# Softmax edge loops of a graph network: two-operand VectorE passes with one operand in PSUM, and two score banks instead of three

## The chip, the core and the metric

The kernel runs on one core of a Trainium2 chip. The core's engines are TensorE (PE, with its weight loads shown as PEld), VectorE (DVE), ScalarE (ACT), GpSimd (POOL) and SyncE (SP); SBUF is the working memory and PSUM the small memory that TensorE writes to. The metric is the device time of one execution in microseconds (us), lower is better.

## The reference

Four graph layers run one after the other on N = 12500 nodes with 64 features and E = 212500 edges sorted by destination. Each layer normalizes the nodes, gathers the source rows along the edges, reduces them per destination, and adds the result to x.

```python
# layer 0: softmax per destination and feature, over the incoming edges
m = relu(feats[src] + edge_h) + EPS
ex = exp(m - segment_max(m, dst)[dst])
a = ex / segment_sum(ex, dst)[dst]
h = segment_sum(m * a, dst)             # then a norm, two linear layers and a batch norm
# layer 1: mean of x[src] per destination, then a linear layer
# layer 2: attention in hyperbolic space (no part of the change)
# layer 3: relational attention, 8 relations x 4 heads
s = leaky_relu(el_all[edge_rel, src] + er_all[edge_rel, dst])
e = exp(s - segment_max(s, dst)[dst])
w = e / segment_sum(e, dst)[dst]
h = segment_sum(feat_all[edge_rel, src] * w, dst)
```

## The kernel before

The edges are padded and cut into two halves, which lie side by side on the partitions (64 features of each half make 128 partitions). A step takes W = 512 edges of each half. There are STEPS = 208 steps in each edge loop. The loops run in series: `softmax_edges(0)`, `mean_edges`, `hyperbolic_edges`, `softmax_edges(3)`, each followed by a stage that works on the nodes. The change touches `softmax_edges` alone, which is built twice: for layer 0 and, with `rel` true, for layer 3.

In every step POOL issues eight indirect DMAs (line 649; four tiles of 128 edges times two halves), each of which gathers 128 rows of a node table by the indices in `idx_all` into one of four slots of `rows`. That makes 1664 gathers in a loop. POOL waits only for the slot: `rows_read` (the same semaphore as `turned`) of four steps before.

The other engines follow, each with its own written-out order of stages with lags in steps:

- PE in layer 0: `to_columns` (lines 764, 766: transposes the rows and the edge features into a bank of `ps_score`), `count` (line 752, counts destinations per bin from `hot`), `to_rows` (line 796, transposes the sums back). In layer 3: `v_columns` (line 775, into `ps_v`), `score_columns` (lines 781 to 788, into `ps_score` and `ps_mult`), `to_rows`.
- DVE in layer 0: `put_in_bins` (line 667), then `segment_sums` of the step two before (lines 713 to 719), then `maxima` of the step before (lines 695 to 707). In layer 3: `own_values` (lines 676, 681), `segment_sums` (lag 3), `maxima` (lag 2).
- ACT: relu or copy of the scores (lines 824, 822), in layer 3 also `widen` (line 813), which waits for the gathered rows; then the exponentials (lines 828, 829), copies out (line 836) and the issue of the stores.
- SP: issues the loads of `attr`, `part_b`, and in layer 3 `v_e` and `marks`.

`maxima` is a running maximum along the edges that starts over at a new destination: `part_b` is 0 inside a segment and very negative where one begins, the scan of line 699 adds it to the running value and takes the maximum with the score, so that `top[:, q, 1:W+1]` holds the maxima after, and `top[:, q, 0:W]` those before, each edge. Lines 704 to 707 then prepare two exponents:

```python
v.tensor_tensor(ps_ex, top[:, q, 0:W], part_b[:, b, :], ALU.add)          # 704
v.tensor_tensor(ex, ps_score[:, c % SCORES, :], top[:, q, 1:W + 1], ALU.subtract)   # 705
v.tensor_tensor(ps_ex, ps_ex, top[:, q, 1:W + 1], ALU.subtract)           # 707
```

`ps_ex` becomes the factor by which the running sums shrink at this edge (zero where a segment begins), `ex` the edge's own weight. `segment_sums` is two scans (716, 719) with `ps_ex` as factor and `ex`, and `ex` times the row, as addends; line 713 makes that product.

Tiles whose names begin with `ps_` lie in PSUM, all others of these loops in SBUF. `slot_free(engine, semaphore, c, ago=n)` makes the engine wait until the step n before has raised the semaphore.

Of the kernel before, what the change touches and what calls it, by code (L numbers as in the profile page):

```python
# [21 lines left out]
ALU = mybir.AluOpType  # L22
ACT = mybir.ActivationFunctionType
# [4 lines left out]
P = 128  # L28
# [48 lines left out]
def build(nc, x, src, dst, edge_attr, edge_type, w0a, b0a, gamma, beta, w0b, b0b, scale0,  # L77
          w1, b1, w2, c2, w3, al3, ar3, b3, out):
    with ExitStack() as whole:
# [455 lines left out]
        def softmax_edges(layer):  # L535
# [3 lines left out]
            rel = layer == 3  # L539
            GW = D + HEADS if rel else D  # L540
            LATER = 1 if rel else 0
            SCORES = 2 if rel else 3
            with nc.cleanup_on_exit(), ExitStack() as ctx:
                def psum(name, shape):
                    return ctx.enter_context(nc.psum_tensor(f"{name}_{layer}", shape, F32))
# [9 lines left out]
                if rel:  # L555
                    v_e = buf("v_e", [P, SLOTS, TILES, HALVES * REL_HEADS])
                    wide = buf("wide", [P, 2, TILES, HALVES * D])
                    marks = buf("marks", [HALVES * REL_HEADS, SLOTS, W, 2], BF16)
                    spread_v = buf("spread_v", [HALVES * REL_HEADS, 2, W])
                    own_v = buf("own_v", [HALVES * REL_HEADS, 2, W])  # L560
                else:
                    attr = buf("attr", [P, SLOTS, HALVES, TILES, D])
# [10 lines left out]
                if not rel:  # L573
                    hot = buf("hot", [P, 2, 2, STREAMS, BLOCKS], BF16)
                    ps_count = psum("ps_count", [P, 2, W])
                    binned, counted, noted = (sem(n) for n in "binned counted noted".split())
                ps_score = psum("ps_score", [P, SCORES, W])
                ps_ex = psum("ps_ex", [P, W])
                ps_out = psum("ps_out", [P, 2, W])
                if rel:  # L580
# [1 line left out]
                    ps_v = psum("ps_v", [HALVES * REL_HEADS, W])  # L582
                got_mask, got_edge, got_rows, put, put_top = ([sem(f"{n}{b}") for b in range(SLOTS)] for n in (
                    "got_mask", "got_edge", "got_rows", "put", "put_top"))
                seeded, v_turned, v_spread, v_own, widened, turned, masked, moved, bent, carried, topped, lowered, diffed, exped, \
                    weighed, summed, back, copied, issue, pe_turn, got_b, parted, powered, merged, m_step, put_cross = (
                        sem(n) for n in (
                            "seeded v_turned v_spread v_own widened turned masked moved bent carried topped lowered diffed exped "
                            "weighed summed back copied issue pe_turn got_b parted powered merged m_step put_cross").split())
                scan_out = scan3 if rel else scan0  # L590
                ROWS = 16 * HALVES * TILES
# [3 lines left out]
                with nc.Block() as block:  # L595
                    @block.sync
                    def _(sp):
                        if rel:
                            first = sp.value_load(cross_i[0:1, 1:2], min_val=0, max_val=HALF - 1)
                            sp.dma_start(spread_v[REL_HEADS:2 * REL_HEADS, 1, W - 1:W],  # L600
                                         at_first[bass.ds(first * HALVES, 1), :].rearrange("a f -> f a"),
                                         allow_slow_non_contiguous=True).then_inc(seeded, 16)

                        def load(c, b, r):
                            if rel:
                                slot_free(sp, v_own, c, ago=SLOTS)
                                sp.dma_start(v_e[:, b, :, :], at_first[bass.ds(c * (W * HALVES), W * HALVES), :].rearrange(
                                    "(p k h) f -> p k (h f)", p=P, k=TILES)).then_inc(got_edge[b], 16)
                                for h in range(HALVES):
                                    sp.dma_start(marks[h * REL_HEADS:(h + 1) * REL_HEADS, b, :, :],  # L610
                                                 mark_row(c + h * STEPS)).then_inc(got_edge[b], 16)
                            else:
                                slot_free(sp, rows_read, c, ago=SLOTS)
                                last = isinstance(c, int) and c == STEPS - 1
                                sp.dma_start(attr[:, b, 0, :, :], edge_rows(edge_attr, c)).then_inc(got_edge[b], 16)
                                sp.dma_start(attr[:, b, 1, :, :], edge_rows(tail, 0) if last else
                                             edge_rows(edge_attr, c + STEPS)).then_inc(got_edge[b], 16)
                            slot_free(sp, diffed, c, ago=SLOTS)
                            sp.sem_inc(issue, 1)
                            for h in range(HALVES):  # L620
                                sp.dma_start(part_b[h * D:(h + 1) * D, b, :],
                                             row(part, c + h * STEPS).broadcast_to([D, W])).then_inc(got_mask[b], 16)

                        written_out(STEPS, (1, load))
                        for b in range(SLOTS):
                            sp.wait_ge(put[b], 32 * (STEPS // SLOTS))
                            sp.wait_ge(put_top[b], 16 * (STEPS // SLOTS))

                        last_b = sp.value_load(cross_i[0:1, 0:1], min_val=HALF, max_val=EP - 1)
                        sp.dma_start(state_b[:, 0:1], max_b[:, bass.ds(last_b - HALF, 1)],  # L630
                                     allow_slow_non_contiguous=True).then_inc(got_b, 16)
                        for j in range(2):
                            sp.dma_start(state_b[:, 1 + j:2 + j],
                                         scan_out[bass.ds(last_b, 1), j * D:(j + 1) * D].rearrange("a f -> f a"),
                                         allow_slow_non_contiguous=True).then_inc(got_b, 16)
                        sp.wait_ge(merged, 1)
                        for j in range(2):
                            sp.dma_start(scan_out[bass.ds(last_b, 1), j * D:(j + 1) * D].rearrange("a f -> f a"),
                                         joined[:, j:j + 1], allow_slow_non_contiguous=True).then_inc(put_cross, 16)
                        sp.wait_ge(put_cross, 32)  # L640
# [15 lines left out]
                    def _(dve):  # L656
# [2 lines left out]
                        v.memset(top[:, 1, W:W + 1], NEG).then_inc(seeded, 1)  # L659
                        v.memset(sums[:, 1, :, W - 1:W], 0.0).then_inc(seeded, 1)  # L660
                        if rel:
                            v.memset(spread_v[0:REL_HEADS, 1, W - 1:W], 0.0).then_inc(seeded, 1)
                        dve.wait_ge(seeded, 19 if rel else 2)

                        def put_in_bins(c, b, r):
                            slot_free(dve, counted, c)
                            v.tensor_tensor(hot[:, b % 2, :, :, :].rearrange("p t j b -> p (t j) b"),  # L667
                                            bins[:, None, :].broadcast_to([P, 2 * STREAMS, BLOCKS]),
                                            cat[:, :, bass.ds(c + BLOCKS, 1)].broadcast_to([P, PARTS, BLOCKS]),
                                            ALU.is_equal).then_inc(binned, 1)  # L670

                        def own_values(c, b, r):
                            dve.wait_ge(got_edge[b], r * 48 + 48)
                            dve.wait_ge(v_turned, c + 1)
                            slot_free(dve, v_spread, c, ago=1)
                            v.tensor_tensor_scan(out=spread_v[:, b % 2, :], data0=marks[:, b, :, 0], data1=ps_v[:, :],
                                                 initial=spread_v[:, 1 - b % 2, W - 1:W], op0=ALU.mult, op1=ALU.add) \
                                .then_inc(v_spread, 1)
                            dve.wait_ge(v_spread, c + 1)
                            slot_free(dve, turned, c)  # L680
                            v.scalar_tensor_tensor(own_v[:, b % 2, :], marks[:, b, :, 1], rel_of[:, :], spread_v[:, b % 2, :],
                                                   ALU.is_equal, ALU.mult).then_inc(v_own, 1)

                        def maxima(c, b, r):
# [16 lines left out]
                            dve.wait_ge(topped, c + 1)  # L701
                            dve.wait_ge(carried, c + 1)
                            slot_free(dve, summed, c, ago=1)
                            v.tensor_tensor(ps_ex[:, :], top[:, q, 0:W], part_b[:, b, :], ALU.add).then_inc(lowered, 1)
                            v.tensor_tensor(ex[:, :], ps_score[:, c % SCORES, :], top[:, q, 1:W + 1], ALU.subtract)
                            dve.wait_ge(lowered, c + 1)
                            v.tensor_tensor(ps_ex[:, :], ps_ex[:, :], top[:, q, 1:W + 1], ALU.subtract).then_inc(diffed, 1)

                        def segment_sums(c, b, r):
                            q = b % 2  # L710
# [36 lines left out]
                    def _(pe):  # L747
# [21 lines left out]

                        def v_columns(c, b, r):  # L770
                            pe.wait_ge(got_edge[b], r * 48 + 48)
                            slot_free(pe, v_spread, c, ago=1)
                            pe.sem_inc(pe_turn, 1)
                            for k in range(TILES):
                                mm = nc.tensor.transpose(ps_v[:, k::TILES], v_e[:, b, k, :], ident[:, :])
# [30 lines left out]
                    def _(act):  # L806
# [19 lines left out]
                        def exps(c, b, r):  # L826
                            act.wait_ge(diffed, c + 1)
                            a.activation(ex[:, :], ex[:, :], ACT.Exp)
                            a.activation(ps_ex[:, :], ps_ex[:, :], ACT.Exp).then_inc(exped, 1)
                            act.dma_start(max_b[:, bass.ds(c * W, W)], top[D:P, b % 2, 1:W + 1]).then_inc(put_top[b], 16)  # L830

                        def copy_out(c, b, r):
# [1376 lines left out]
```

## Time and profile before

| | |
|---|---|
| median of 3 runs | 10075.73 us (10074.14 to 10075.74) |
| span of the profiled execution, first to last instruction | 10045.6 us |
| the profiled execution's own time | not given apart from its span |
| busy share of the span | POOL 73%, DVE 69%, PE 66%, ACT 42% |
| first softmax loop (layer 0), first to last gather | 232.2 to 2359.4 us |
| mean loop (layer 1), first to last gather | 2670.4 to 4748.6 us |
| last softmax loop (layer 3), first to last gather | 7712.3 to 9839.6 us |

Busy shares are averages over stages with different limits. A group's row gives a line, an engine and an operation, what it writes and reads, how often it ran, its busy time and mean duration, and the idle time of the engine just before it with what ended that idle time. "issue" there means that the engine waited for nothing that the profile shows. In the timeline each row has a start in us, a duration in us, and in brackets the idle time before it.

### The profile page before, as it was taken

Reading aid. Unit: us, or ns where it says so; the run is one execution under the profiler, and the core shown is the slowest. Engines: PE = TensorE matmul, PEld = TensorE weight load, DVE = VectorE, ACT = ScalarE, POOL = GpSimd, SP = SyncE. Lnnn points to the kernel's source line nnn. Section 1 sums busy time; section 2 is a strip of 40 time slices with the busy share of each in tenths; the row PEclk is TensorE's granted clock in tenths of the full one; section 3 lists DMA queues with packets and bytes.
Section 4 is the critical chain, followed back from the end, with each engine's and each line's share of the span. In section 5 each row is a group of like instructions: output and inputs, shape, how many; then the busy total and the mean of one; then the engine's idle time right before and its main releaser. Section 6 shows DMA issues by size and latency. Waiting matters only on the chain. (4 is left out here: it accounts for less than half of the span.)

```text
span 10045.6 us, 120472 instructions
## 1 busy us (share of the span) xinstructions
PE 6609.3 (66%) x28159; PEld 5230.6 (52%) x28159; DVE 6940.6 (69%) x14143; ACT 4170.6 (42%) x8456; POOL 7317.4 (73%) x7482
## 2 busy tenths in 40 slices
PE   0777777774436566665548888888856776677661
PEld 0444444442235555555448888888854444455441
DVE  4666666666656666663667777777764888888885
ACT  0222222221236666666236666666644333333330
POOL 5777777776477777776877777777756777777775
PEclk9665555565568888888555555555557567655775
DMA  4444444444422222222245555555545444444442
GB/s 99 123 129 129 130 128 130 128 130 78 151 66 66 67 66 66 66 66 62 19 95 106 106 106 106 106 106 106 106 108 150 132 128 132 129 131 129 131 130 72
DMA packets 1318230, 1059.32 MB, mean 105 GB/s; under 512 B 815857, under 2 KB 1034376, under 8 KB 1316531
## 3 DMA queue, kind: packets, MB, share of 16 engines
q0 software_dynamic: 238720, 318.69, 15.9%
q1 hardware_dynamic: 681698, 373.56, 14.5%
q10 hardware_dynamic: 397397, 362.35, 11.0%
q8 instruction: 161, 2.64, 0.1%
q14 instruction: 254, 2.08, 0.1%
HBM read 580.99 MB, written 472.73 MB: 105 GB/s over the span
## 5 line engine op out<-in xcount | busy, mean ns | idle before, releaser
L1173 POOL DMA_INDIRECT h_rows_d<-table,h_idx_d x1840 | 1750.4, 951 | 568.5 <-issue 560.5
L649 POOL DMA_INDIRECT rows<-table,idx_all x1664 | 1621.7, 975 | 527.6 <-issue 506.8
L649 POOL DMA_INDIRECT rows<-table3s,idx_all x1664 | 1621.8, 975 | 518.5 <-issue 506.7
L956 POOL DMA_INDIRECT m_rows<-table,idx_all x1664 | 1572.5, 945 | 507.0 <-issue 507.0
L986 PE MATMUL m_ps_sort<-m_hot_high,m_hot_low 128*128 128x224 f32 x3328 | 936.1, 453 | 621.1 <-DVE m_hot_high L1080 516.0
L986 PEld LDWEIGHTS m_ps_sort<-m_hot_high,m_hot_low 128*128 128x128 f32 x3328 | 822.0, 252 | 706.3 <-DVE m_hot_high L1080 547.6
L1193 PE MATMUL h_ps_sum<-h_rows_d,h_hot 128*128 128x65 f32 x3680 | 818.7, 412 | 324.8 <-DVE h_rows_d L1330 324.8
L764 PE MATMUL ps_score<-ident,rows 128*128 128x128 f32 x1664 | 655.7, 498 | 567.5 <-DMA rows<-table,idx_all 559.2
L1193 PEld LDWEIGHTS h_ps_sum<-h_rows_d,h_hot 128*128 128x128 f32 x3680 | 782.6, 323 | 409.9 <-issue 409.9
L796 PE MATMUL ps_out<-ident,sums 128*128 128x128 f32 x3328 | 714.3, 384 | 281.8 <-DVE sums L719 281.7
L764 PEld LDWEIGHTS ps_score<-ident,rows 128*128 128x128 f32 x1664 | 417.3, 312 | 826.2 <-issue 826.2
L796 PEld LDWEIGHTS ps_out<-ident,sums 128*128 128x128 f32 x3328 | 627.4, 222 | 417.9 <-DVE sums L719 362.0
L1049 DVE TENSOR_TENSOR_SCAN m_sums<-m_same_b,m_sums,m_ps_rows 128x512 f32<-128x512 bf16 x208 | 266.2, 1280 | 826.6 <-issue 637.5
L1211 PE MATMUL h_ps_src<-h_near,h_hot_t 128*128 128x65 f32 x3680 | 829.8, 417 | 2.5 <-ACT h_hot_t L1235 2.5
L1211 PEld LDWEIGHTS h_ps_src<-h_near,h_hot_t 128*128 128x128 f32 x3680 | 809.7, 332 | 3.2 <-issue 3.2
L824 ACT ACTIVATE ps_score<-ps_score 128x512 f32<-128x512 f32 x208 | 121.1, 582 | 1611.4 <-PE ps_score L766 1611.4
L813 ACT ACTIVATE wide<-rows 128x256 f32<-128x256 f32 x416 | 149.9, 407 | 1485.9 <-DMA rows<-table3s,idx_all 1485.9
L1339 DVE SCALAR_TENSOR_TENSOR h_run<-h_run,h_goes_on,h_ps_sum 128x65 f32<-128x65 f32 x1840 | 518.5, 282 | 233.4 <-PE h_ps_sum L1193 5.0
L1024 ACT ACTIVATE m_hot_low<-m_hot_low,record,m_slope 128x128 f32<-128x128 f32 x1664 | 660.0, 480 | 6.1
L667 DVE TENSOR_TENSOR hot<-bins,cat 128x784 bf16<-128x784 bf16 x208 | 202.8, 976 | 647.1 <-PE ps_count L752 647.0
L1088 DVE SCALAR_TENSOR_TENSOR m_junk<-cat,m_ps_base 128x98 f32<-128x98 f32 (+61 forms) x1664 | 586.7, 419 | 0.0
L766 PE MATMUL ps_score<-ident,attr 128*64 128x128 f32 x3328 | 578.0, 448 | 0.0
(425 smaller groups left out, 14380.2 us busy)
## 6 DMA issues: line engine op xcount, KB each, us to landing
scan<-out_e ACTq DMA_DIRECT2D x832, 256.0 KB, 3.2
h_near<-table SPq DMA_DIRECT2D x1840, 32.5 KB
run_g<-h_run ACTq DMA_DIRECT2D x230, 260.0 KB
part_b<-part SPq DMA_DIRECT2D x832, 64.0 KB
max_b<-top ACTq DMA_DIRECT2D x416, 128.0 KB
scan<-m_out_e SPq DMA_DIRECT2D x416, 128.0 KB
attr<-in_edge_attr SPq DMA_DIRECT2D x415, 128.0 KB
h_rows_d<-table,h_idx_d POOLq DMA_INDIRECT x1840
```

The lines of the kernel that those rows point to most:

```text
L649: pool.indirect_dma_start(out=rows[:, b, k, h * GW:(h + 1) * GW], out_offset=None, in_=table3s.rearrange("n (q f) -> (n q) f", f=HEADS) if ...
L764: nc.tensor.matmul(ps_score[:, c % SCORES, k::TILES], rows[:, b, k, :], ident[:, :], start=True, stop=False)
L766: mm = nc.tensor.matmul(ps_score[h * D:(h + 1) * D, c % SCORES, k::TILES], attr[:, b, h, k, :], ident[:, :], start=False, stop=True)
L796: mm = nc.tensor.transpose(ps_out[:, j, k * P:(k + 1) * P], sums[:, b % 2, j, k::TILES], ident[:, :])
L956: pool.indirect_dma_start(out=rows[:, b, k, h * D:(h + 1) * D], out_offset=None, in_=table1, in_offset=bass.IndirectOffsetOnAxis(ap=idx_al ...
L986: nc.tensor.matmul(ps_sort[:, 0:SORTED], hot_low[:, w % 2, j, :], hot_high[:, w % 2, j, :], start=n == 0, stop=n == PC - 1).then_inc(place ...
L1024: ins = a.activation(hot_low[:, w % 2, j, :], hot_low[:, w % 2, j, :], ACT.Relu, bias=record[:, at:at + 1], scale=slope[:, at:at + 1])
L1088: v.scalar_tensor_tensor(junk[:, at % 4, 0:BLOCKS + n], cat[:, p, 0:BLOCKS + n], cat[:, p, BLOCKS + n:BLOCKS + n + 1], ps_base[:, 0:BLOCKS ...
L1173: pool.indirect_dma_start(out=rows_d[:, b, k, :], out_offset=None, in_=table2, in_offset=bass.IndirectOffsetOnAxis(ap=idx_d[:, c * BT + k: ...
L1193: mm = nc.tensor.matmul(ps_sum[:, k // HB, (k % HB) * ACC2:(k % HB + 1) * ACC2], hot[:, b, k, :], rows_d[:, b, k, D + 1:ROW2], start=True, ...
L1211: mm = nc.tensor.matmul(ps_src[:, k // HB, (k % HB) * (D + 1):(k % HB + 1) * (D + 1)], hot_t[:, b % 2, k * P:(k + 1) * P], near[:, b, k, : ...
L1339: v.scalar_tensor_tensor(run[:, b, k, :], before, goes_on[:, bass.ds(c * BT + k, 1)], ps_sum[:, k // HB, (k % HB) * ACC2:(k % HB + 1) * AC ...
```

## The change

In `softmax_edges`, for both layers, some passes of DVE read or write PSUM where they read or wrote SBUF.

- Line 667 (`put_in_bins`, layer 0) compares with the bin numbers in a new PSUM bank `ps_bins`, filled once ahead of the loop. To make room, `ps_score` has two banks in layer 0 as well, as it has in layer 3. So `to_columns` of step c waits for line 713 of step c-2 instead of c-3.
- Line 704 subtracts the maximum before from the score in PSUM instead of adding `part_b` to it; line 707 takes the maximum of minus `part_b` and that difference. `ps_ex` is then the negative of what it was, and ACT's exponential (line 829) multiplies by -1.
- Lines 676 and 681 (`own_values`, layer 3): the scan writes in place into `ps_v` instead of `spread_v`, a copy keeps its last column in `v_last` for the next step, and line 681 reads `ps_v`. `v_columns` on PE waits for that copy and for line 681 of the step before, where it waited for the scan.

```diff
-            SCORES = 2 if rel else 3
+            SCORES = 2
...
-                    spread_v = buf("spread_v", [HALVES * REL_HEADS, 2, W])
+                    v_last = buf("v_last", [HALVES * REL_HEADS, 1])
...
+                    ps_bins = psum("ps_bins", [P, W])[:, 0:BLOCKS]
...
-                            sp.dma_start(spread_v[REL_HEADS:2 * REL_HEADS, 1, W - 1:W],
+                            sp.dma_start(v_last[REL_HEADS:2 * REL_HEADS, :],
...
-                            v.memset(spread_v[0:REL_HEADS, 1, W - 1:W], 0.0).then_inc(seeded, 1)
-                        dve.wait_ge(seeded, 19 if rel else 2)
+                            v.memset(v_last[0:REL_HEADS, :], 0.0).then_inc(seeded, 1)
+                        else:
+                            v.tensor_copy(ps_bins, bins[:, :]).then_inc(seeded, 1)
+                        dve.wait_ge(seeded, 19 if rel else 3)
...
                             v.tensor_tensor(hot[:, b % 2, :, :, :].rearrange("p t j b -> p (t j) b"),
-                                            bins[:, None, :].broadcast_to([P, 2 * STREAMS, BLOCKS]),
+                                            ps_bins[:, None, :].broadcast_to([P, 2 * STREAMS, BLOCKS]),
                                             cat[:, :, bass.ds(c + BLOCKS, 1)].broadcast_to([P, PARTS, BLOCKS]),
                                             ALU.is_equal).then_inc(binned, 1)
...
-                            slot_free(dve, v_spread, c, ago=1)
-                            v.tensor_tensor_scan(out=spread_v[:, b % 2, :], data0=marks[:, b, :, 0], data1=ps_v[:, :],
-                                                 initial=spread_v[:, 1 - b % 2, W - 1:W], op0=ALU.mult, op1=ALU.add) \
-                                .then_inc(v_spread, 1)
+                            slot_free(dve, v_kept, c, ago=1)
+                            v.tensor_tensor_scan(out=ps_v[:, :], data0=marks[:, b, :, 0], data1=ps_v[:, :],
+                                                 initial=v_last[:, :], op0=ALU.mult, op1=ALU.add).then_inc(v_spread, 1)
                             dve.wait_ge(v_spread, c + 1)
+                            v.tensor_copy(v_last[:, :], ps_v[:, W - 1:W]).then_inc(v_kept, 1)
                             slot_free(dve, turned, c)
-                            v.scalar_tensor_tensor(own_v[:, b % 2, :], marks[:, b, :, 1], rel_of[:, :], spread_v[:, b % 2, :],
+                            v.scalar_tensor_tensor(own_v[:, b % 2, :], marks[:, b, :, 1], rel_of[:, :], ps_v[:, :],
                                                    ALU.is_equal, ALU.mult).then_inc(v_own, 1)
...
-                            v.tensor_tensor(ps_ex[:, :], top[:, q, 0:W], part_b[:, b, :], ALU.add).then_inc(lowered, 1)
+                            v.tensor_tensor(ps_ex[:, :], ps_score[:, c % SCORES, :], top[:, q, 0:W], ALU.subtract).then_inc(lowered, 1)
                             v.tensor_tensor(ex[:, :], ps_score[:, c % SCORES, :], top[:, q, 1:W + 1], ALU.subtract)
                             dve.wait_ge(lowered, c + 1)
-                            v.tensor_tensor(ps_ex[:, :], ps_ex[:, :], top[:, q, 1:W + 1], ALU.subtract).then_inc(diffed, 1)
+                            v.scalar_tensor_tensor(ps_ex[:, :], part_b[:, b, :], -1.0, ps_ex[:, :], ALU.mult, ALU.max).then_inc(diffed, 1)
...
-                            slot_free(pe, v_spread, c, ago=1)
+                            slot_free(pe, v_kept, c, ago=1)
+                            slot_free(pe, v_own, c, ago=1)
...
-                            a.activation(ps_ex[:, :], ps_ex[:, :], ACT.Exp).then_inc(exped, 1)
+                            a.activation(ps_ex[:, :], ps_ex[:, :], ACT.Exp, scale=-1.0).then_inc(exped, 1)
```

## Rows read from the trace of the kernel before

**Rows 1.** Page of the profile: span, and share of each engine.

```profile
span 10045.6 us, 120472 instructions
...
PE 6609.3 (66%) x28159; PEld 5230.6 (52%) x28159; DVE 6940.6 (69%) x14143; ACT 4170.6 (42%) x8456; POOL 7317.4 (73%) x7482
```

**Rows 2.** Page, costliest groups: POOL's gathers of the softmax and mean loops.

```profile
L649 POOL DMA_INDIRECT rows<-table,idx_all x1664 | 1621.7, 975 | 527.6 <-issue 506.8
L649 POOL DMA_INDIRECT rows<-table3s,idx_all x1664 | 1621.8, 975 | 518.5 <-issue 506.7
L956 POOL DMA_INDIRECT m_rows<-table,idx_all x1664 | 1572.5, 945 | 507.0 <-issue 507.0
```

**Rows 3.** Gathers by line: ns min/median/max, first and last start; who waited.

```profile
L649 POOL DMA_INDIRECT rows<-table,idx_all x1664: 940/945/1712, 232.2 to 2359.4; - x185
L649 POOL DMA_INDIRECT rows<-table3s,idx_all x1664: 940/945/1461, 7712.3 to 9839.6; - x185
...
  ACT wide L813: 1485.9, 208
  PE ps_score L764: 559.2, 206
...
L956 POOL DMA_INDIRECT m_rows<-table,idx_all x1664: 940/945/1922, 2670.4 to 4748.6; - x185
```

**Rows 4.** Timeline of the first softmax loop, two steps.

```profile
1203.21 1.27 DVE L716 TENSOR_TENSOR_SCAN sums<-ps_ex,sums,ex 128x512 f32<-128x512 f32 x1
...
1203.91 0.95 POOL L649 DMA_INDIRECT rows<-table,idx_all  x1 [0.30 <-issue]
...
1212.38 0.98 DVE L667 TENSOR_TENSOR hot<-bins,cat 128x784 bf16<-128x784 bf16 x1 [3.56 <-PE ps_count L752]
...
1212.66 1.51 POOL L649 DMA_INDIRECT rows<-table,idx_all  x1 [0.30 <-issue]
1213.27 0.68 DVE L713 TENSOR_TENSOR weighted<-ex,ps_score 128x512 f32<-128x512 f32 x1
...
1215.87 0.77 PE L764 MATMUL ps_score<-ident,rows 128*128 128x128 f32 x2 [1.82 <-DMA rows<-table,idx_all]
```

**Rows 5.** Timeline of the last softmax loop, two steps.

```profile
8702.87 0.70 DVE L704 TENSOR_TENSOR ps_ex<-top,part_b 128x512 f32<-128x512 f32 x1
8703.19 1.18 POOL L649 DMA_INDIRECT rows<-table3s,idx_all  x1 [0.30 <-issue]
...
8705.98 0.74 DVE L681 SCALAR_TENSOR_TENSOR own_v<-marks,rel_of,spread_v 64x512 f32<-64x512 bf16 x1
...
8709.16 1.27 DVE L716 TENSOR_TENSOR_SCAN sums<-ps_ex,sums,ex 128x512 f32<-128x512 f32 x1
...
8709.68 0.94 POOL L649 DMA_INDIRECT rows<-table3s,idx_all  x1 [0.30 <-issue]
...
8713.44 1.06 PE L775 MATMUL ps_v<-ident,v_e 128*64 128x128 f32 x4
...
8716.65 0.74 DVE L681 SCALAR_TENSOR_TENSOR own_v<-marks,rel_of,spread_v 64x512 f32<-64x512 bf16 x1
...
8717.16 1.04 POOL L649 DMA_INDIRECT rows<-table3s,idx_all  x1 [0.30 <-issue]
```

**Rows 6.** Groups by form, DVE in the first softmax loop (232 to 2361 us).

```profile
L667 DVE TENSOR_TENSOR hot<-bins,cat 128x784 bf16<-128x784 bf16 x208 | 202.8, 976 | 647.1 <-PE ps_count L752 647.0
L704 DVE TENSOR_TENSOR ps_ex<-top,part_b 128x512 f32<-128x512 f32 x206 | 144.2, 700 | 7.0
```

**Rows 7.** Groups by form, DVE in the last softmax loop (7712 to 9841 us).

```profile
L676 DVE TENSOR_TENSOR_SCAN spread_v<-marks,spread_v,ps_v 64x512 f32<-64x512 bf16 x208 | 262.3, 1261 | 12.8 <-PE ps_v L775 12.8
...
L707 DVE TENSOR_TENSOR ps_ex<-ps_ex,top 128x512 f32<-128x512 f32 x206 | 141.9, 689 | 0.0
L713 DVE TENSOR_TENSOR weighted<-ex,ps_mult 128x512 f32<-128x512 f32 x205 | 141.0, 688 | 289.3 <-ACT ps_ex L829 289.3
...
L695 DVE COPY top<-top 128x1 f32<-128x1 f32 x206 | 30.5, 148 | 0.0
```

More of the change, by code:

```diff
@@ L584, in softmax_edges @@
                     "got_mask", "got_edge", "got_rows", "put", "put_top"))
-                seeded, v_turned, v_spread, v_own, widened, turned, masked, moved, bent, carried, topped, lowered, diffed, exped, \
+                seeded, v_turned, v_spread, v_kept, v_own, widened, turned, masked, moved, bent, carried, topped, lowered, diffed, exped, \
                     weighed, summed, back, copied, issue, pe_turn, got_b, parted, powered, merged, m_step, put_cross = (
                         sem(n) for n in (
-                            "seeded v_turned v_spread v_own widened turned masked moved bent carried topped lowered diffed exped "
+                            "seeded v_turned v_spread v_kept v_own widened turned masked moved bent carried topped lowered diffed exped "
                             "weighed summed back copied issue pe_turn got_b parted powered merged m_step put_cross").split())
```

## The prediction

> **What bounds the kernel now.** I read the page first: GpSimd (POOL) has the largest busy share, 73% of a 10045.6 us span [rows 1]. A share over the whole span says little, since the kernel is a row of stages, so I went on to the costliest groups. The three edge loops with 1664 gathers each are to be set beside each other there [rows 2]. The two softmax loops (line 649, once with table, once with table3s) and the mean loop between them (line 956) issue the same number of indirect DMAs of the same shape pattern. POOL's busy time is 1621.7, 1621.8 and 1572.5 us, and the idle time that is put down to "issue" is the same in all three (506.8, 506.7, 507.0 us).
>
> Two things follow. First, POOL never waits for anyone inside these loops: busy plus issue is 2128.5 us for the first softmax loop, and its gathers run from 232.2 to 2359.4 us, which is 2127.2 us from first to last start [rows 3]. The consumers wait for POOL: PE 206 times for rows in the first loop (559.2 us), ScalarE 208 times in the last (1485.9 us) [rows 3]. So the pace of both loops is the gather issue, 2127.2 / 208 = 10.23 us a step of eight gathers. Second, gathers cost 30 ns more on average in the softmax loops (975 against 945). The median is 945 in all three, while the longest in the softmax loops are 1712 and 1461 ns [rows 3]: a few gathers are stretched a lot, the rest not at all.
>
> The timeline tells which. In the first loop a gather that starts at 1212.66 takes 1.51 us, while the bin pass of line 667 (both operands in SBUF) runs from 1212.38 to 1213.36; the gather ends 0.81 us after that pass [rows 4]. In the last loop a gather at 8703.19 takes 1.18 us and ends at 8704.37, 0.80 us after the pass of line 704 (top and part_b, both SBUF) ended at 8703.57. One at 8717.16 ends at 8718.20, 0.81 us after line 681 (marks and spread_v, both SBUF) [rows 5]. Three different passes, one distance: an ordinary gather of 0.945 us is held some 0.13 us into its run until the pass ends, then needs its remaining 0.81.
>
> Other passes don't do this. The scan of line 716 (ps_ex from PSUM, ex from SBUF) covers 1203.21 to 1204.48, and the gather that starts inside it at 1203.91 takes 0.95 [rows 4]. In the last loop it covers 8709.16 to 8710.43, and the gather at 8709.68 takes 0.94 [rows 5]. Both were at their 0.13 us point inside a long VectorE pass with one operand in PSUM.
>
> **The change, part by part.** The passes of these loops with both tensors in SBUF are 667 and 704 in the first loop, 704 and 681 in the last; each gets one operand from PSUM. Line 704 reads ps_score instead of part_b, and part_b moves to line 707, whose other operand is ps_ex. Nothing else in either loop reads two SBUF tensors, so I expect the stretching to go.
>
> The gain: each softmax loop falls to what the mean loop pays for as many gathers, 1621.7 - 1572.5 = 49.2 us in the first and 1621.8 - 1572.5 = 49.3 us in the last, together 98.5 us [rows 2]. Bounds: the mean loop has some stretched gathers of its own (its longest is 1922 ns, 0.98 us above the median [rows 3]), so a loop with none could be 1 to 2 us better: at most some 102 us in all. On the other side the copy of one column, line 695 (148 ns [rows 7]), and its new sister for v_last remain. What line 695 costs is in the 49 us already, as it runs before and after. Were each new copy to hold a gather for its whole length whenever the two meet, that is 0.15 us in at most 0.148/1.25 = 12% of 208 steps, 1.25 us being the distance of two unstretched gathers (945 ns and 507.0/1664 = 0.305 us of issue): 4 us. So 94 to 102 us, and 98.5 taken, as the mean loop is the nearest row.
>
> What the edits cost on VectorE. Pass for pass the number of elements stays. A pass from two SBUF tensors (704) has a mean of 700 ns, and one of the same size with an operand in PSUM (713) 688; in place in PSUM (707) it is 689 [rows 6, 7]. So I price the moved operands at nothing, with 10 ns either way as bound. The scan in place in ps_v isn't in the trace; the nearest are line 676 (1261 ns, PSUM operand, SBUF out) and 707 (in place, no penalty) [rows 7], so 1261 is taken, and at the far end twice that. New in the last loop is the v_last copy between scan and own_v: 0.15 us, plus a wait on the scan that own_v had anyway. VectorE's slack there: 289.3 us of waiting for ps_ex over 208 steps [rows 7], 1.39 us a step, so its work is 10.23 - 1.39 = 8.84 us. With the copy 8.99, against a new step of 2078.5 / 208 = 9.99 us. It stays hidden, by 1.0 us; a scan of twice the length would eat that and 0.26 us more, 54 us over the loop, taking the last loop's gain away. In the first loop the slack is larger, 647.1 us before line 667 alone [rows 6]. The seed copy of bins into PSUM happens once, while POOL is already gathering: nothing.
>
> Two score banks: the transposes of step c now wait for line 713 of step c-2 instead of c-3. Behind that wait on PE stand the count and to_rows matmuls of the older steps. In the timeline line 713 of c-2 ends at 1213.95, and the transposes of c start at 1215.87, released by the gather's landing [rows 4]. The new wait is over 1.9 us before it would hold anyone, 1.7 with a step 0.24 us shorter: nothing. If the cover were gone, PE would be late, and POOL only after four row slots more.
>
> ps_v stays one bank, held until own_v (line 681) instead of until the scan. Line 681 of one step ends at 8706.72, and the next transposes into ps_v (line 775) start at 8713.44 [rows 5], because to_rows, ahead of them on PE, waits for a later VectorE pass. 6.7 us of cover: nothing. The DMAs keep number and size; part_b is held until line 707 (diffed), which still comes last.
>
> **The sum.** The loops stand in series with the stages between them, so what POOL saves is saved at the end: span 10045.6 - 98.5 = 9947.1 us. The profiled execution's own time isn't given; the median of the runs, 10075.73, lies 30.1 us above its span, which I take as around the span and unchanged. 10075.7 - 98.5 = 9977.2 us.
>
> **Rivals.** *Half the gain.* One of the rewritten passes still holds gathers: line 667, whose other operand is a broadcast column of cat, or line 681 with its per-partition rel_of beside marks. Against it: the scans too read a start value per partition from SBUF and held nothing. One loop keeps at most its 49 us: 10026 us, chance 0.05.
>
> *No change.* It isn't the second SBUF operand that holds the gather but VectorE work as such, or the gather's own landing. For it: no row shows a bin pass with a PSUM operand. Against it: the covering scans [rows 4, 5], and the constant 0.8 us after three kinds of pass. The time stays at 10076, chance 0.04. The Trainium skill (SBUF — State Buffer, section Who interferes with whom) would be split here. It says that a VectorE instruction with two SBUF inputs contends with a GpSimd instruction that reads SBUF and not with one that only writes; it adds, as inferred, that descriptor generation needs the write interface, so that a tensor_tensor pass didn't stall DMAs in its probe. By that last remark the change would give nothing; the stretched gathers in the timeline speak for the first.
>
> *Slower.* VectorE becomes the pace of the last loop through the in-place scan in PSUM. It decides from 1.0 us a step beyond the copy (no gain left in that loop from 1.24). At three times 1261 ns, VectorE's step is 8.99 + 2.52 = 11.51 us: 208 x (11.51 - 10.23) = +266, less 49 in the first loop, 10293 us. Line 707's 689 ns in place speaks against it. Chance 0.03.
>
> **How the numbers follow.** Forecast 0.88. Its own range is 9973 (102 us) to 9982 (94 us); with 4 us for runs and for the drain of a pipeline that ends differently below, and 10 above for stretched gathers that come back where the phase of POOL against VectorE shifts, 9969 to 9992. The rivals (0.12) are left out of it. A change of 0.2%, 20 us, is about what this kernel's measurement tells from nothing. Faster by more: 0.88 + 0.05 = 0.93; within: 0.04; slower: 0.03.
>
> **What would show it.** Right: the two line 649 groups at a mean near 945 ns, busy near 1572 us, the issue idle still 507; hardly a gather over 1 us; the first mean-loop gather some 49 us earlier, the last softmax loop ending some 98 us earlier; line 667 near 976 ns, the v_last copy near 0.15 us; ScalarE still waiting for rows in the last loop, VectorE still waiting before line 713, though less. Wrong: POOL at 975 ns (no change) or at 945 in one loop only (half); POOL idle on "turned" (VectorE or PE sets the pace); a PE wait for line 713 in the first loop; a scan in ps_v well above 1.26 us.

## The result, and the profile after

The changed kernel takes 9958.77 us (median of 4 runs, 9956.82 to 9959.68) against 10075.74 us before: 117.0 us less, ratio 0.9885 with an interval of 0.9873 to 0.9896. The forecast was 9977.2, with 9969 to 9992 as its range. The sign and the mechanism held; the gain was larger than the range allowed. The page of the changed kernel answers to [rows 1, 2], with the gathers of the loop of line 1173 (now 1177) beside them, which the prediction had not listed:

```profile
span 9957.7 us, 120683 instructions
...
L1177 POOL DMA_INDIRECT h_rows_d<-table,h_idx_d x1840 | 1764.4, 959 | 569.3 <-issue 560.5
L650 POOL DMA_INDIRECT rows<-table,idx_all x1664 | 1571.0, 944 | 527.6 <-issue 506.5
L650 POOL DMA_INDIRECT rows<-table3s,idx_all x1664 | 1571.0, 944 | 518.7 <-issue 506.9
L960 POOL DMA_INDIRECT m_rows<-table,idx_all x1664 | 1572.4, 945 | 507.0 <-issue 507.0
```

Both softmax loops now issue their gathers at the mean loop's price, with the same issue idle as before. By line, in ns (shortest, median, longest), with first and last start and those who waited:

```profile
L650 POOL DMA_INDIRECT rows<-table,idx_all x1664: 940/945/962, 233.3 to 2310.2; - x185
L650 POOL DMA_INDIRECT rows<-table3s,idx_all x1664: 940/945/991, 7675.5 to 9752.4; - x185
...
  ACT wide L817: 1435.1, 208
  PE ps_score L767: 633.4, 198
```

The longest gather is 962 and 991 ns where it was 1712 and 1461 [rows 3]: no gather over 1 us is left in either loop. The loops take 2076.9 us each from first to last start, 50.3 and 50.4 us less than in the trace of before. The consumers still wait for rows.

A count over the whole trace of before bears out what the single rows of the prediction suggest. 119 gathers of the first loop and 209 of the last run more than 15 ns above their median. What they take above it adds up to 50.4 and 50.3 us, all that the two loops have lost since. Of the 119, 117 end 0.81 to 0.83 us after a pass of line 667; of the 209, 167 end 0.80 to 0.82 us after one of line 704 and 38 after one of line 681.

So the two traces account for 100.7 us in these loops, yet the spans differ by 10045.6 - 9957.7 = 87.9 us and the medians by 117.0 us. Two things stand in between. One lies in the trace: the loop of line 1173, which the change doesn't touch, became longer. Its row in the trace of before, then in the one after:

```profile
L1173 POOL DMA_INDIRECT h_rows_d<-table,h_idx_d x1840: 940/945/1337, 5129.3 to 7439.3; - x184
```

```profile
L1177 POOL DMA_INDIRECT h_rows_d<-table,h_idx_d x1840: 940/945/1312, 5079.5 to 7403.4; - x184
```

2310.0 us became 2323.9, 13.9 more; 100.7 - 13.9 = 86.8, and the stages between give the remaining 1.1. The other lies outside: the profiled execution after took 9959.39 us, 1.7 us above its span, while the runs of before lie 30.1 us above the span of the trace of before.

VectorE in the last softmax loop after, by form (mean ns in the middle, idle before it at the end), answers to [rows 7]:

```profile
L679 DVE TENSOR_TENSOR_SCAN ps_v<-marks,v_last,ps_v 64x512 f32<-64x512 bf16 x208 | 264.8, 1273 | 12.5 <-PE ps_v L779 12.5
...
L684 DVE SCALAR_TENSOR_TENSOR own_v<-marks,rel_of,ps_v 64x512 f32<-64x512 bf16 x208 | 151.5, 729 | 0.0
...
L716 DVE TENSOR_TENSOR weighted<-ex,ps_mult 128x512 f32<-128x512 f32 x205 | 141.0, 688 | 225.9 <-ACT ps_ex L833 225.8
...
L682 DVE COPY v_last<-ps_v 64x1 f32<-64x1 f32 x208 | 31.2, 150 | 7.1
```

The scan in place costs 1273 ns (1261 before), the new copy 150, and VectorE still waits 225.9 us before the product.

### The profile page after: what moved, and what is told of

The parts are those of the page before. It is cut to its first block and busy times, and to the rows that moved or that the text cites. A ratio compares the mean times of both kernels' runs of the same rounds, so it can differ in the third digit from the quotient of the medians.

```text
span 9957.7 us, 120683 instructions
## 1 busy us (share of the span) xinstructions
PE 6444.3 (65%) x28159; PEld 5147.3 (52%) x28159; DVE 6950.2 (70%) x14352; ACT 4171.1 (42%) x8456; POOL 7230.9 (73%) x7482
## 5 line engine op out<-in xcount | busy, mean ns | idle before, releaser
L650 POOL DMA_INDIRECT rows<-table,idx_all x1664 | 1571.0, 944 | 527.6 <-issue 506.5
L650 POOL DMA_INDIRECT rows<-table3s,idx_all x1664 | 1571.0, 944 | 518.7 <-issue 506.9
L767 PE MATMUL ps_score<-ident,rows 128*128 128x128 f32 x1664 | 582.7, 447 | 638.7 <-DMA rows<-table,idx_all 633.4
L767 PEld LDWEIGHTS ps_score<-ident,rows 128*128 128x128 f32 x1664 | 368.0, 276 | 873.7 <-issue 873.7
L670 DVE TENSOR_TENSOR hot<-ps_bins,cat 128x784 bf16<-128x784 f32 x208 | 202.3, 973 | 590.1 <-PE ps_count L755 590.0
L719 DVE TENSOR_TENSOR_SCAN sums<-ps_ex,sums,ex 128x512 f32<-128x512 f32 x416 | 531.1, 1277 | 0.0
```

Source lines behind the costliest of these rows:

```text
L650: pool.indirect_dma_start(out=rows[:, b, k, h * GW:(h + 1) * GW], out_offset=None, in_=table3s.rearrange("n (q f) -> (n q) f", f=HEADS) if ...
L719: v.tensor_tensor_scan(out=sums[:, q, 0, :], data0=ps_ex[:, :], data1=ex[:, :], initial=sums[:, 1 - q, 0, W - 1:W], op0=ALU.mult, op1=ALU.add)
L767: nc.tensor.matmul(ps_score[:, c % SCORES, k::TILES], rows[:, b, k, :], ident[:, :], start=True, stop=False)
```

## The experiments

The kernel before was timed on the chip of each experiment too, and chips differ: on one the unstretched gather has a median of 944 ns, on another 947. So runs are set beside before, or beside the changed kernel, on the same chip; the mean loop, which no kernel here touches, tells how a chip counts. The loop lengths below are from first to last start of the gathers, worked out before rounding, so they can differ by 0.1 us from the rows.

**The kernel before, once more.** No edit.

> The unchanged kernel, profiled once more. Theory 1 (the profiled execution of before was a short one, and how many gathers are stretched differs from execution to execution): spans near 10074 us, some 2 us below each run's time, and a trace with some 28 us more of stretched gathers than the first trace, in the softmax loops, in the loop of line 1173, or in both. Theory 2 (some 30 us really lie around the span of before, and the change shortened them): a span near 10046 us again, with runs near 10076.

Measured: a run takes 10063.45 us with a span of 10061.7. In all its 10 runs the time is 1.7 to 1.8 us above the span, and they lie between 10056.23 and 10067.45. Its page:

```profile
L1173 POOL DMA_INDIRECT h_rows_d<-table,h_idx_d x1840 | 1761.1, 957 | 569.3 <-issue 560.7
L649 POOL DMA_INDIRECT rows<-table,idx_all x1664 | 1624.0, 976 | 527.7 <-issue 506.9
L649 POOL DMA_INDIRECT rows<-table3s,idx_all x1664 | 1626.2, 977 | 518.3 <-issue 506.9
L956 POOL DMA_INDIRECT m_rows<-table,idx_all x1664 | 1571.5, 944 | 507.2 <-issue 506.9
```

The three loops take 2129.8, 2320.8 and 2131.7 us, where the first trace had 2127.3, 2310.0 and 2127.3: 17.7 us more, 10.8 of them in the loop of line 1173, and the span is 16.1 longer. No 30 us lie around the span. Theory 1 is right that the first trace was of a short execution; the 28 us expected on top came out as 16 on this chip.

**Layer 0 alone and layer 3 alone.** The first keeps the old lines for `rel`, the second for layer 0; of the edits one is shown.

```diff
-            v.tensor_tensor(ps_ex[:, :], top[:, q, 0:W], part_b[:, b, :], ALU.add).then_inc(lowered, 1)
+            if not rel:     # in the second kernel: if rel
+                v.tensor_tensor(ps_ex[:, :], ps_score[:, c % SCORES, :], top[:, q, 0:W], ALU.subtract).then_inc(lowered, 1)
+            else:
+                v.tensor_tensor(ps_ex[:, :], top[:, q, 0:W], part_b[:, b, :], ALU.add).then_inc(lowered, 1)
```

> The change in layer 0 alone. Theory 1 (a gather is held by a pass with two SBUF tensors): the first softmax loop from first to last gather at 2077 us with hardly a gather over 1 us, the last softmax loop as in before (2127 us or somewhat more, with the stretched gathers at lines 704 and 681); time about half of the gain, 10005 to 10030 us. Rival (the gain needs both layers, or comes from another stage): no gain in this loop, 10076 us; or all of it, 9959.

> The change in layer 3 alone, layer 0 as before with three score banks. Theory 1: first softmax loop 2127 us or somewhat more, last softmax loop 2077 us; time 10005 to 10030 us, and the two savings of this run and of the run with layer 0 alone add up to the whole, 117 us, within some 15 us that the loop of line 1173 can swing. Rival (the pieces interact): the sum misses 117 us by over 20.

Measured: 10006.06 us (ratio 0.9946, interval 0.9929 to 0.9962) and 10011.24 us (0.9948, 0.9932 to 0.9965), against 10060.71 for before on the same chip. The gathers, layer 0 alone, then layer 3 alone:

```profile
L650 POOL DMA_INDIRECT rows<-table3s,idx_all x1664 | 1628.8, 979 | 518.3 <-issue 506.8
L650 POOL DMA_INDIRECT rows<-table,idx_all x1664 | 1570.1, 944 | 527.7 <-issue 506.6
```

```profile
L649 POOL DMA_INDIRECT rows<-table,idx_all x1664 | 1630.4, 980 | 527.5 <-issue 506.8
L649 POOL DMA_INDIRECT rows<-table3s,idx_all x1664 | 1570.2, 944 | 518.4 <-issue 507.0
```

Each part frees its own loop and no other. The savings are 54.7 and 49.5 us, 104.1 together, 13 short of the 117, which was not measured on this chip; that is within the bound set. The untouched loop stands at 979 and 980 ns here, 2134.7 and 2136.0 us, more than in the two traces of before shown so far.

**The score differences alone.** Lines 704 and 707 and the sign of the exponential as changed, in both loops; bins, `own_values` and three banks as before.

> Only the score differences (lines 704, 707 and the exponential's sign) in both loops; bins, own_values and the three banks as before. Theory 1: stretched gathers remain at line 667 in the first loop, which stays near 2127 us, since nearly all of them stood at 667 there; in the last loop those at 704 (36 of 51 us) go and those at 681 (14 us) stay, or grow as the phase shifts: 2090 to 2115 us. Time 10035 to 10065 us. Rival (704 is as costly in the first loop): first loop below 2110 us.

Measured: 10008.85 us (0.9951, interval 0.9934 to 0.9967).

```profile
L649 POOL DMA_INDIRECT rows<-table,idx_all x1664 | 1626.5, 977 | 527.8 <-issue 506.9
L649 POOL DMA_INDIRECT rows<-table3s,idx_all x1664 | 1570.7, 944 | 519.1 <-issue 507.1
```

Theory 1 holds for the first loop, where 704 was not the cost (2132.4 us). For the last loop I was wrong, and with it for the time: with 704 rewritten the loop takes 2076.8 us, though line 681 still reads two SBUF tensors. Three gathers of it are held at line 681, for 0.4 us in all.

**The changed kernel beside three variants of it.** On this chip before takes 10061.81 us. First the changed kernel unaltered:

> The changed kernel once more, beside the others of this call. Both softmax loops at 2076 to 2077 us from first to last gather, spans some 1.75 us under the times, and little spread, since nothing holds a gather there any more. On a chip where before takes 10061 us I expect 9948 to 9960.

Measured: 9949.91 us (ratio 0.9887, interval 0.9870 to 0.9903), softmax loops 2076.1 and 2076.3 us, the loop of line 1177 2319.6 us. The little spread did not come: the four runs lie between 9945.51 and 9956.05.

**One extra pass with two SBUF operands, and the same pass with one in PSUM.** Ahead of the bin pass of the first loop:

```diff
+                            slot_free(dve, extra, c, ago=1)
+                            v.tensor_tensor(extra_c[:, :, :], extra_a[:, None, :].broadcast_to([P, 3, W - P]),
+                                            extra_b[:, None, :].broadcast_to([P, 3, W - P]), ALU.add).then_inc(extra, 1)
```

In the second kernel `extra_b` is replaced by columns of the bank of `ps_bins`.

> The changed kernel with one more pass a step in the first softmax loop, ahead of the bin pass: 1152 elements (some 1.35 us), both operands in SBUF, its result unused. VectorE waits 590 us in that loop, 2.8 us a step, so the pass itself has room. Theory 1 (a gather at its sensitive point waits for the end of a pass with two SBUF operands): the pass is longer than the 1.25 us between gathers, so it meets at least one in nearly every step; held by 0.1 to 1.35 us each, the loop becomes 20 to 280 us longer, some 150 if the phases are spread evenly, and the stretched gathers end 0.82 us after this pass. Rival (it was the length of VectorE's work, or the wait for counts): the same as with the extra pass whose operand is in PSUM.

> The same extra pass of 1152 elements, with its second operand read from the free columns of the PSUM bank of the bins. Theory 1: no gather is held; the first loop stays at 2077 us and the time within 5 us of the changed kernel. Rival (any long VectorE pass holds gathers, or VectorE's time sets the pace): the loop as long as with the SBUF pass.

Measured: 10072.92 us with both operands in SBUF, 9949.89 with one in PSUM. Of the SBUF kernel, the gathers' row of the page, then VectorE's and POOL's timeline around one extra pass; after it the same three views of the PSUM kernel:

```profile
L656 POOL DMA_INDIRECT rows<-table,idx_all x1664 | 1687.3, 1014 | 527.8 <-issue 506.9
```

```profile
1210.01 1.35 DVE L679 TENSOR_TENSOR extra_c<-extra_a,extra_b 128x1152 f32<-128x1152 f32 x1
```

```profile
1211.00 1.18 POOL L656 DMA_INDIRECT rows<-table,idx_all  x1 [0.30 <-issue]
```

```profile
L656 POOL DMA_INDIRECT rows<-table,idx_all x1664 | 1570.1, 944 | 527.8 <-issue 506.9
```

```profile
1207.30 1.35 DVE L679 TENSOR_TENSOR extra_c<-extra_a,ps_bins 128x1152 f32<-128x1152 f32 x1
```

```profile
1207.80 0.94 POOL L656 DMA_INDIRECT rows<-table,idx_all  x1 [0.30 <-issue]
```

Same length, same place, same engine: the pass with two SBUF operands adds 123 us (117.1 in its loop, 2193.2 against 2076.1), the one with a PSUM operand nothing. In the trace of the SBUF kernel 203 gathers are stretched in that loop; all of them end 0.81 to 0.83 us after the extra pass, and what they take above the median is the 117.1 us. In the rows above, the SBUF pass ends at 1211.36 and its gather at 1212.18, 0.82 us apart as in [rows 4, 5]; in the other kernel the gather starts half a microsecond into the pass and runs as ever. This settles it against the rival that VectorE work as such holds gathers.

**The loop of line 1173, too.** That loop has one long pass with two SBUF tensors, the product of the gathered rows and their weights (line 1334 after, 1330 before); its others are of 8 columns and 0.17 us. In the trace of the changed kernel, VectorE and POOL:

```profile
6002.35 0.69 DVE L1334 TENSOR_TENSOR h_rows_d<-h_rows_d,h_weight 128x520 f32<-128x520 f32 x1
```

```profile
6002.76 1.10 POOL L1177 DMA_INDIRECT h_rows_d<-table,h_idx_d  x1 [0.30 <-issue]
```

The pass ends at 6003.04, the gather at 6003.86: 0.82 us again. The edit puts the weights into the bank of PSUM that this loop leaves free, once on top of the changed kernel and once on the kernel before:

```diff
-                weight = buf("weight", [P, 2, BT])
+                ps_weight = psum("ps_weight", [P, W])[:, 0:BT]
...
-                            slot_free(act, messaged, c)
+                            slot_free(act, messaged, c, ago=1)
...
-                            a.activation(weight[:, b % 2, :], ratio[:, b % 2, :], ACT.Exp, scale=inv_sqrt_c[:, :]).then_inc(weighed, 1)
+                            a.activation(ps_weight, ratio[:, b % 2, :], ACT.Exp, scale=inv_sqrt_c[:, :]).then_inc(weighed, 1)
...
-                                            weight[:, b % 2, :, None].broadcast_to([P, BT, ACC2]), ALU.mult).then_inc(messaged, 1)
+                                            ps_weight[:, :, None].broadcast_to([P, BT, ACC2]), ALU.mult).then_inc(messaged, 1)
```

> The changed kernel, and in the loop of line 1173 the weights that multiply the gathered rows lie in PSUM (one buffer for two), so that this pass (line 1330 of before) has one SBUF operand as well. Theory 1 carried over: 27 us of stretched gathers there go, the loop from first to last gather falls from 2320 to 2324 us to 2297 to 2300, and the kernel is 20 to 27 us faster than the changed one. Rival (PE, 88% busy there, or the single weight buffer sets the pace of that loop): no change, or slower, with POOL idle on the semaphore of the add-up matmuls.

> The kernel before with the weights of the loop of line 1173 in PSUM, nothing else changed. The loop falls to 2296 us; the softmax loops stay at 2127 to 2137; time 20 to 27 us under before, some 10038 us where before takes 10061. Rival (that loop's stretching came from the phase that the softmax change leaves): no gain.

Measured: 9927.62 us on top of the change (ratio to before 0.9864, interval 0.9847 to 0.9880), 22.3 us under the changed kernel on the same chip; on the kernel before 10050.00 against 10071.41 (0.9982, 0.9973 to 0.9992), 21.4 us less. One of the ten runs of the latter took 10088.20 us, the others 10046.51 to 10057.81. The loop's gathers, on top of the change and on the kernel before:

```profile
L1177 POOL DMA_INDIRECT h_rows_d<-table,h_idx_d x1840 | 1736.3, 944 | 569.6 <-issue 560.7
```

```profile
L1173 POOL DMA_INDIRECT h_rows_d<-table,h_idx_d x1840 | 1740.4, 946 | 569.8 <-issue 560.9
```

The loop takes 2296.0 us (2319.6 without the edit) and 2300.3 us (2324.2 in the trace of before on that chip, where a gather is 2 to 3 ns longer). The stretching there is its own, not something that the softmax change leaves behind. PE, busy for 1986.5 of 2325 us there in the trace of the changed kernel (85%), did not set the pace.

**A third trace of before, and own_values as before.** The first has no edit; the second undoes the changes to lines 676 and 681 and `v_last` in the changed kernel.

> A third trace of the unchanged kernel. Theory 1 (stretching in before differs from execution to execution, and the first trace was a light one): each time again 1.75 us above its span; the two softmax loops at 2127 to 2137 us and the loop of line 1173 at 2310 to 2325, with sums that differ by several us from both earlier traces. Theory 2 (the first trace's loops are the rule): 2127.3, 2310.0 and 2127.3 us again.

> The changed kernel with own_values as before (scan into spread_v, no copy of the last column, line 681 with two SBUF tensors). From the run with the score differences alone, whose last loop took 2076.8 us: with line 704 gone, VectorE and POOL keep one phase and line 681 meets no gather's sensitive point; last loop 2076 to 2079 us, time within 4 us of the changed kernel (9950 us where before takes 10061). Rival (by the sum of my prediction each rewritten pass saves its part): last loop 2090 us or more, 14 us lost.

Measured: the third trace has 10075.92 us, a span of 10074.2 and loops of 2130.0, 2324.2 and 2135.7 us. With `own_values` as before the time is 9966.33 us against 10071.41 (ratio 0.9896, interval 0.9879 to 0.9912; the whole change had 0.9887 and 0.9885). On this chip every gather is 2 to 3 ns longer, so neither the time nor the loop is to be set beside 9950 and 2076 to 2079; its rows:

```profile
L650 POOL DMA_INDIRECT rows<-table3s,idx_all x1664 | 1574.8, 946 | 518.7 <-issue 507.3
L959 POOL DMA_INDIRECT m_rows<-table,idx_all x1664 | 1575.2, 947 | 507.4 <-issue 507.1
```

The last loop stands at the mean loop's price without that part of the change (2081.1 us, the mean loop 2081.3), as the run with the score differences alone had shown. Four of its gathers are held at `own_values`, for 0.9 us. The rewriting is worth that much in this trace, and nothing that the times can tell.

## Why the prediction was wrong in size and right in kind

**The step that failed** is the one from span to median: "the median of the runs, 10075.73, lies 30.1 us above its span, which I take as around the span and unchanged." In every run of the experiments the time is 1.7 to 1.8 us above that run's own span. The other 28 us said that the profiled execution was shorter than the runs, and stretched gathers, of which the change removes most, are part of what differs between executions. So the term "98.5 us", the gain, was mis-sized: it was read from one short execution and taken from the median of longer ones. For that execution it was nearly right, as the two loops lost 100.7 us from trace to trace. On the chip of the second trace of before the two loops take 2129.8 and 2131.7 us, and 2076.0 and 2076.3 where their own part is changed: 53.8 + 55.4 = 109.2 us. In the times the whole change gives 117.0 us where the result was taken, and 111.9 on the chip where the changed kernel was run again (10061.81 to 9949.91). The bound of 102 us did not hold for the same reason: it was worked out from the stretching of a single execution.

**The first trace.** From it, 9947.1 us was forecast as the span and 9957.7 came: 13.9 us for the loop of line 1173, -2.2 for the two softmax loops and -1.1 elsewhere. Of the 28 us that it lay under the runs, that loop can hold 9 to 14, since it takes 2319 to 2324 us in every other trace with its weights in SBUF, before and after the change alike. If it held 14 in the runs too, the other 14 would put the gain of the two softmax loops at 115 us, near the 117.0 measured. That is an estimate: these runs have no trace. It asks for softmax loops no longer than others that were seen, as the untouched ones of the runs with one layer changed, 2136.0 and 2134.7 us, are 118 us together above the changed ones. Where the 28 us lay stays open. The record doesn't name the chip of the first trace, and part of them could be a difference of chips: before has a median of 10060.71 us on one and 10071.41 on another.

**The gain's mechanism** held: a gather reaches, about 0.13 us into its run, a point at which it waits for the end of a VectorE pass with two SBUF tensors. The pair of extra passes shows the operand to be the cause, and the pass in the loop of line 1173 keeps the same 0.82 us. The Trainium skill (SBUF — State Buffer, section Who interferes with whom) says that a VectorE instruction with two SBUF inputs contends with a GpSimd instruction that reads SBUF; the 123 us between the extra passes agree. Its remark, marked there as inferred, that descriptor generation needs the write interface, so that a tensor_tensor pass didn't stall DMAs in its probe, does not carry over to these gathers: lines 667 and 704 and the extra pass, all of that form, held them.

Two SBUF tensors are not the only way to hold a gather. The longest gather of the mean loop, 1922 ns [rows 3], ends 0.82 us after a pass with a single SBUF input, here in the trace of before:

```profile
2671.69 1.92 POOL L956 DMA_INDIRECT m_rows<-table,idx_all  x1 [0.30 <-issue]
```

```profile
2671.78 1.01 DVE L1038 TENSOR_SCALAR m_slope<-record 128x1664 f32<-128x1664 f32 x1
```

The pass ends at 2672.79, the gather at 2673.61. There is one such gather in each trace of this loop, 1.0 us of the 1.4 that its stretched ones cost, so neither this change nor the forecast hangs on it.

**That each rewritten pass had to go** was wrong for line 681. Whether a pass holds a gather depends on where it stands against POOL's beat of 1.25 us. In the trace of before, line 681 held a gather after none of the 166 passes of line 704 that held one, and after 37 of the 39 that held none. The steps of [rows 5] show one of each kind, with these rows beside theirs:

```profile
8705.93 0.94 POOL L649 DMA_INDIRECT rows<-table3s,idx_all  x1 [0.30 <-issue]
...
8713.43 0.94 POOL L649 DMA_INDIRECT rows<-table3s,idx_all  x1 [0.30 <-issue]
8713.55 0.70 DVE L704 TENSOR_TENSOR ps_ex<-top,part_b 128x512 f32<-128x512 f32 x1
```

The gather held at 704 ends at 8704.37; the one from 8705.93 on meets line 681 (from 8705.98) and takes its usual 0.94 us. In the step after, 704 holds none, and 681 holds the gather from 8717.16 on. So the two take turns: after a hold at 704 a gather reaches its sensitive point less than 0.1 us behind line 681's start, and it is not held. With 704 rewritten the sensitive point comes 1.0 to 1.1 us after 681's start in most steps, when the pass of 0.74 us is over, so line 681 holds three or four gathers in the whole loop. So the two shares of the last loop, 36 us at 704 and 14 at 681, could not be added as if each pass stood alone. Why the steps settle at 1.0 to 1.1 us stays open, and whether line 704 had to be rewritten in the first loop was not tried: with 667 as before it held 1 to 4 gathers there.

**The covers** held. The scan in place cost 12 ns more, the copy 150 ns as priced, and VectorE kept 225.9 us of waiting in the last loop. In the first loop no PE wait for the product line stands among the waits of the changed kernel with two banks; the bin pass took 973 ns (976 before). The one-column copies, for which the prediction allowed 4 us, left no gather over 991 ns. None of the rivals came in.

**The spread** says little. It is 11.2 us over 10 runs of before, 2.9 and 10.5 us over four runs each of the changed kernel, and 2.2 us over four runs with the weights in PSUM as well (9926.02 to 9928.18), where no loop of VectorE passes stretches the gathers noticeably. That the last is small because the stretching is gone fits, but is not shown by so few runs.

## What to carry to other kernels

Where GpSimd's indirect DMAs set the pace, read the longest of a group beside its median, and look which VectorE pass ends a fixed time before each stretched one. Moving one operand of that pass to PSUM cost VectorE nothing here (973 ns against 976, 1347 against 1353) and gave the whole stretch back. A pass that is out of step with the gathers costs next to nothing (0.4 and 0.9 us for line 681), so try the passes one by one before rewriting all. And when the runs lie well above the profiled span, profile the kernel once more before calling the difference fixed: the trace may be of a shorter execution, and what varies may be part of the size that is to be forecast.

## What the hardware showed that I had not expected

- Loops with the same instructions differ from trace to trace: on one chip, with one gather median (944 ns), the first softmax loop as before took 2129.8, 2132.4 and 2136.0 us. Over all traces with its weights in SBUF the loop of line 1173 took 2310.0 to 2324.2 us; its stretched gathers took 13 us above the median in the first trace and 22 to 27 in the others.
- Chips differ in the gather itself: medians of 944, 945 and 947 ns, some 4 us over a loop of 1664 (mean loop 2077.3 to 2081.4 us).
- A VectorE pass of 1353 ns a step, with its operands in SBUF, lengthened the loop by 117.1 / 208 = 0.56 us a step; the same pass with a PSUM operand, 1347 ns, by nothing.
